# A local-attention layer pipelined over five engines: other token-block pairing, another PSUM bank and another engine for parts of the feed-forward norm, and a new order of work

## What is computed

```python
for i in range(6):
    x = attn_layer(shift_tokens(x), Wqkv[i], q_scale[i], k_scale[i], Wo[i]) + x
    x = ffn_layer(shift_tokens(x), ln_g[i], ln_b[i], W1[i], b1[i], W2[i], b2[i]) + x
# shift_tokens: the second half of the features comes from the token before
# attn_layer: q, k, v = x @ Wqkv; q and k to unit length per head, scaled, rotated;
#   each window of 32 attends to itself and the window before (masked softmax); @ Wo
# ffn_layer: xn = (x - mu) / sqrt(var + 1e-5) * g + b; a, gate = split(xn @ W1 + b1)
#   return a * gelu(gate) @ W2 + b2          (W1: 128 x 682, W2: 341 x 128)
```

## Time and profile before

| | |
|---|---|
| median of 3 runs | 4047.65 us (4046.55 to 4050.84) |
| the profiled execution | 4048.09 us, its span 4046.3 us |
| TensorE busy | 3729.9 us, 92% of the span |
| VectorE busy | 3487.8 us, 86% |
| ScalarE busy | 3422.3 us, 85% |
| GpSimd busy | 2387.8 us, 59% |
| mean granted TensorE clock | 0.982 of full |

### The profile page before, as it was taken

How to read it: one execution, slowest core, us unless ns; L and a number is a source line. 1 busy time by engine, 2 the same in 40 slices (tenths; PEclk the granted TensorE clock), 3 DMA queues, 4 the chain that set the end, 5 groups by cost and what they waited for, 6 DMA issues and landing times.

```text
span 4046.3 us, 125302 instructions
## 1 busy us (share of the span) xinstructions
PE 3729.9 (92%) x49248; PEld 2338.2 (58%) x49248; DVE 3487.8 (86%) x7192; ACT 3422.3 (85%) x9269; POOL 2387.8 (59%) x1420
## 2 busy tenths in 40 slices
PE   5999999967999999999999999999999999998987
PEld 2444444434666666666666666666666666666665
...
GB/s 50 8 9 9 9 9 36 1 0 50 80 76 77 90 85 81 75 80 86 87 82 74 80 77 95 85 77 77 76 98 80 79 76 75 98 82 79 76 82 56
DMA packets 158791, 263.19 MB, mean 65 GB/s; under 512 B 45696, under 2 KB 72064, under 8 KB 157952
## 3 DMA queue, kind: packets, MB, share of 16 engines
...
## 4 chain that ended last, share of the span: by engine, by line
PE 62%; DVE 18%; ACT 12%; issue 3%; POOL 2%; SPq 1%; DMA 1%; DVEq 0%; POOLq 0%; ACTq 0%
PE ps L655 17%; ACT arena L931 6%; PE ps L601 5%; PE ps L596 5%; PE ps L688 5%; PE ps L724 5%; PE ps L542 4%; PE ps L733 4%; PE ps L762 3%; PE ps L709 3%; PE ps L768 3%; DVE ssq L1164 3%; PE ps L537 3%; PE ps L775 3%; DVE arena L1147 2%
## 5 line engine op out<-in xcount | busy, mean ns | idle before, releaser
L655 PE MATMUL ps<-WB,arena 128*128 128x512 f32 x2304 | 1110.5, 605 | 132.5 <-DVE arena L1244 61.4
L931 ACT ACTIVATE arena<-arena,nmx 128x64 f32<-128x64 f32 x3072 | 1020.1, 337 | 4.4 <-DVE arena L1222 3.8
L475 POOL TENSOR_TENSOR arena<-arena 128x1024 f32<-128x1024 f32 x192 | 454.4, 2367 | 516.3 <-DVE arena L1147 516.0
L655 PEld LDWEIGHTS ps<-WB,arena 128*128 128x128 f32 x2304 | 399.9, 192 | 463.2 <-issue 438.8
L907 ACT ACTIVATE arena<-ps 128x1024 f32<-128x1024 f32 x384 | 393.5, 1025 | 314.1 <-PE ps L655 307.7
L491 POOL TENSOR_TENSOR arena<-arena,rinv 128x1024 f32<-128x1024 f32 x192 | 365.2, 1902 | 389.9 <-DVE rinv L1195 389.9
L931 ACT ACTIVATION_READ_ACCUMULATOR arena<-arena,nmx 128x1 f32 x3072 | 584.3, 190 | 0.0
L1141 DVE TENSOR_TENSOR arena<-ps,tables 128x1024 f32<-128x1024 f32 x384 | 464.7, 1210 | 87.4 <-ACT arena L907 87.4
L688 PEld LDWEIGHTS ps<-ident,arena 128*128 128x128 f32 x3072 | 355.6, 141 | 239.1 <-issue 173.6
L1147 DVE TENSOR_TENSOR arena<-ps,tables 128x512 f32<-128x512 f32 x768 | 489.9, 678 | 0.0
L480 POOL TENSOR_TENSOR arena<-arena 128x1024 f32<-128x1024 f32 x192 | 455.1, 2371 | 30.8 <-DVE arena L1147 30.8
...
## 6 DMA issues: line engine op xcount, KB each, us to landing
arena<-arena SPq DMA_DIRECT2D x768, 128.0 KB, 2.3
...
WB<-wb SPq DMA_DIRECT2D x24, 512.0 KB, 5.0
...
arena<-Y SPq DMA_DIRECT2D x96, 128.0 KB, 2.4
...
```

Of the source, the lines that this page charges most:

```text
L475: pool.tensor_tensor(tu[:, K], t1[:, K], t2[:, K], ALU.add).then_inc(addk_r, 1)
L655: i = pe.matmul(banks[:, c, :], xs_[t % RING], WB[:, w * INNER + c * COL:w * INNER + (c + 1) * COL], start=True, stop=True)
L931: i = act.activation(pe3[:, :, h, :], sc[:, 64 * h:64 * h + 64].rearrange("p (k q) -> p k q", k=2), ACT.Exp, bias=nmx[:, h:h + 1], accum_o ...
```

## The change

1. **Block pairing.** Side 0 serves blocks 0 and 2, side 1 blocks 1 and 3. Side 1 then needs the tile's values as they are, so `values` is one copy of 128 rows; side 0 needs them with the last 32 rows from the tile before, which two DMAs build. `outputs` writes in runs of 32 floats instead of 64.
2. **Bank.** The feed-forward's turn, back and down use bank 7 (attention's second output bank) between `outputs` of a tile and `attend` of the next. Gate and value products stay in banks 2 and 3. The waits move from `queries_of` to `attend`.
3. **Norm.** The unit step moves from VectorE to ScalarE, as scale and shift; VectorE adds one negation of the means, GpSimd one product.
4. **Order.** All five lists are reordered: attention's products come right behind the keys' of the next step, the value copy behind twelve of the sixteen exponents, the last four exponents between the second and the third gelu, the sine part of K before the cosine part. `add_k` and `add_q` are split over two steps. Weights of a new layer are issued behind `vshift` and `ff_in`. Feed-forward lags grow by one.

```diff
-        FF_BANK = 2, 3
+        FF_BANK, FO_BANK = (2, 3), 7
...
-                    q, o = slice(WIN * w, WIN * (w + 1)), (WIN * w + 64) % P
-                    here = slice((w % 2) * COL, (w % 2 + 1) * COL)
-                    sp.dma_start(PTw[q, w // 2, here], pt[q, COL:2 * COL]).then_inc(wide_in, 16)
+                    q, o = slice(WIN * w, WIN * (w + 1)), (WIN * w + 96) % P
+                    here = slice((w // 2) * COL, (w // 2 + 1) * COL)
+                    sp.dma_start(PTw[q, w % 2, here], pt[q, COL:2 * COL]).then_inc(wide_in, 16)
...
-                for dst, side, src, row, held in ((64, 0, (t - 1) % RING, 96, 1), (96, 0, r, 0, 0), (0, 1, r, 32, 0),
-                                                  (32, 1, r, 64, 1)):
-                    sp.dma_start(vv[r][dst:dst + WIN, side, :], vv[src][row:row + WIN, held, :])\
-                        .then_inc(vs_in, 16)
+                sp.dma_start(vv[r][0:96, 0, :], vv[r][0:96, 1, :]).then_inc(vs_in, 16)
+                sp.dma_start(vv[r][96:P, 0, :], vv[(t - 1) % RING][96:P, 1, :]).then_inc(vs_in, 16)
...
             def queries_of(t):
-                need(pe, rotq_r, t)
-                for q, lag, count, each in ((chunk(t - 2, 7), 7, fn_r, 1), (chunk(t - 2, 8), 8, xn_r, 1),
-                                            (chunk(t - 2, 9), 9, hf_r, MF), (chunk(t - 2, 10), 10, fin_r, 1)):
-                    if q is not None:
-                        pe.wait_ge(count, each * (q + 1))
+                need(pe, rotq_r, 2 * t)
+                q = chunk(t - 2, 10)
+                if q is not None:
+                    pe.wait_ge(hf_r, MF * (q + 1))
...
             def attend(t):
+                for q, count in ((chunk(t + 2, 8), fn_r), (chunk(t + 2, 9), xn_r), (chunk(t + 2, 11), fin_r)):
+                    if q is not None:
+                        pe.wait_ge(count, q + 1)
...
-            def values(t, side):
-                rows = slice(64 * side, 64 * side + 64)
-                i = act.activation(vv[t % RING][rows, side, :], kv_ps[rows].rearrange("p b c -> p (b c)"), ACT.Copy)
+            def values(t):
+                act.wait_ge(v_mm, t + 1)
+                need(act, vs_in, 32 * (t - 1))
+                act.activation(vv[t % RING][:, 1, :], kv_ps.rearrange("p b c -> p (b c)"), ACT.Copy).then_inc(v_r, 1)
+
+            def ff_unit(q):
+                act.wait_ge(frs_r, 2 * q + 2)
+                for j in range(PER):
+                    i = act.activation(fx[:, j * P:(j + 1) * P], ps[:, FO_BANK, j * P:(j + 1) * P], ACT.Identity,
+                                       bias=shift[:, j:j + 1], scale=rstd[:, 0, j:j + 1])
+                i.then_inc(fn_r, 1)
```

230 lines of the change are left out of this document (116 added, 114 removed).

## The result

The changed kernel takes **4025.7 us** (median of 6 runs, 4022.7 to 4035.6) against 4050.3 (6 runs, 4046.6 to 4051.4): a ratio of 0.9944, 95% interval 0.9932 to 0.9957. It is faster, by 24.6 us or 0.6%, small but clear of the scatter, where 88 us were forecast. The profiled execution has a span of 4021.9 us. Its page, first part: busy us, share of the span, instructions.

The account below looks back on a forecast made before the run. A ring of waits through ScalarE's value copy, not one full engine, was taken to bound the new order. From 4048.09 us: -98 for groups, +7.5 for layers, +3 for the end, about -88, so 3960; range 3928 to 4034.

Parts of the forecast that it names:

- the ring: Plain step: key products through attention, ScalarE's copies and exponents to the value copy, which releases the next key product: 13.64 us.
- (a): Rival, gate step between gelu 1 and 2: added table switches cost double, 63.5 per group, about 4062 us; chance 0.07.
- (e): Rival, value copy: one copy over 128 partitions costs like two, 2.03 us; group 64.3, about 4105 us; chance 0.02.
- (b): Rival, attention's products: the "issue" stall stays in full, hidden nowhere; group 62.3, about 4008 us; chance 0.14.
- (c): Rival, back step: VectorE closes its own ring, transpose waits for GpSimd's scaling; group 62.8, about 4033 us; chance 0.09.
- signs of being right: Key products in three of four steps idle 1 to 1.2 us for the value copy; group near 61.3; TensorE's work unchanged.
- signs of being wrong: Down-step query product released by VectorE's hidden product, transpose by GpSimd, attention's products by a DMA, or groups below 60.5.
- -2.04, times 48 is -98: Main term: each group of four tiles falls from 63.34 to 61.3 us, over 48 groups.
- Such an operation took 0.75 beside GpSimd: VectorE's added scaling of the mean, turn step: taken as 0.2, upper end 0.8, not charged because VectorE waits for exponents.
- I take 0.2: Per-group charge for the 1.18 us "issue" stall inside attention's products, bounds 0 and 1.2.
- +7.5: Five layer changes: key product waits for later-issued weights, 4.3 us lost per layer against 2.8 before, +1.5 each.
- bounds 0 and +6, taken as +3: End of the kernel: same chain with one stage moved, at most one group's gate and value products no longer beside attention.

Follow-up runs that it names:

- Experiments 13 and 14: Changed kernel with the scaling of the mean moved from VectorE to GpSimd: 4023.3 us; with the addition to the variance moved there too: 4016.6 us.
- Experiment 9: Changed kernel with the end reordered: gate and value products of the last chunk but one ahead of the last tile's attention: 4012.3 us.
- experiment 1: Changed kernel with a new layer's key and query weights issued right behind the widening DMAs again: 4011.1 us.

## Why the prediction was right in direction and wrong in size

**Right.** The single copy over 128 rows costs half, a table switch 1.28, TensorE's work is unchanged, and the value copy closes the ring in the new order. Turn, gate and down step came out at 13.78, 18.7 and 15.15 against 13.64, 18.50 and 15.25. Table switches (a) and the full-price copy (e) were rightly set low: the gelu starts 0.02 us behind the load, with no drain.

The 4025.7 us lie in the stated range, 3928 to 4034, because it was drawn to hold rivals (b) and (c), and mechanisms of both were at work; as a forecast of 3960 it missed by 66. Of the signs of being right, one failed: the value copy holds the key product in two steps of the group, by about 0.6 us, and not in three by 1 to 1.2. Of the signs of being wrong one came: a transpose released by GpSimd.

**The step that failed first: "-2.04, times 48 is -98".** Measured: -1.35 undisturbed and +0.28 of what lies beyond (13.5 over 47.75), -1.07 in all. The missing 0.97 are, up to rounding, 0.29 of the starting point, 0.38 of one small operation, 0.20 of other links by which the steps are longer than laid out (0.14 of it in the turn step), and 0.08 beyond the 0.2 that were taken for stalls. The last is small only because two things cancel: the groups between lose 0.54 more than before, the first and last ones 0.26 less, which the forecast didn't have.

- The group it started from, 63.34 us, is the typical one but not an undisturbed one: 63.05 is. The 0.29 between them is scattered stall or the like (the 35 groups between lose 0.32 each), and I counted it among what the new ring would save: 14 us. A laid-out ring knows no stalls, so it must be set against a group without any, and the stalls carried over as a term of their own.
- "Such an operation took 0.75 beside GpSimd; I ... charge neither, because in that step VectorE waits for the exponents anyway." The scaling of the mean took 1.22 us, and the cover was not there: the mask starts right behind the roots, at 16.6 from the step's key product, later than the 16.3 laid out. Late roots made GpSimd's scaling of the keys late, behind which stands that of the probabilities; it ends at 2080.37, the transpose starts 0.03 later, 6.8 into the back step and not 6.4, and the exponents follow at 8.1 and not 7.67. This is rival (c)'s link, a transpose waiting for GpSimd, at 0.31 us rather than the 1.5 of the earlier trace rows. Experiments 13 and 14 show it: take both small operations away, and the back step is 13.78. That is 0.38 per group, 18 us. The row that I used for the price, 754 ns, was itself such a wait: in the trace of before that operation starts at 2003.58 and ends at 2004.33, GpSimd's scaling of the keys at 2004.31. It was no price of an operation but what was left of another engine's. The two rows of before:

```profile
2003.58 0.75 DVE L1239 TENSOR_SCALAR ve<-mv 128x4 f32<-128x4 f32 x1
2002.41 1.90 POOL L491 TENSOR_TENSOR arena<-arena,rinv 128x1024 f32<-128x1024 f32 x1 [2.04 <-DVE rinv L1195]
```

**The issue stalls: "I take 0.2".** The term, 10 us, was too small. In the 35 groups between, 37.0 us or 1.06 a group lie beyond the undisturbed group, where 11.2 or 0.32 lay before, with as much stalling (23.6 against 24.4 us). The sum of the scattered part (+13.5) looks like the forecast's 10 only because the last 19 tiles gained 10 us, for a reason that no run looks into. The reason given for hiding, "it falls in the 1.15 us that TensorE now waits for the value copy", failed in its size: the copy is awaited for only 0.5 to 0.7 us, in two steps, and a stall is up to 2.5. The 1.15 was laid out for a plain step, and the group has none: the turn and the back step each have 0.6 us of the feed-forward's own turns in that place, as the layout itself says of the turn step. "There are now gaps in which the fetch can catch up" failed as well, since scores are still 256 instructions without one. Rival (b), stalls in full and hidden nowhere, 1.2 a group, had both the mechanism and about the size.

**Layers: +7.5, measured +12.0.** The mechanism was right: TensorE waits 3.7 to 4.1 us for weights, five times. Before, 3.6 us were lost at each and not the 2.8 taken, and after 6.0 and not 4.3, since some fetch stalls fall into these groups too. Issued early, the weights are there, and the tables on VectorE are next.

**End: "bounds 0 and +6, taken as +3", measured +13.3.** The step that failed was "the same chain with one stage moved". The stage moved behind the last tile's attention, which itself waits 3.8 us for its transfers; so the gate step stood between that attention and the last chunk's turn, with nothing beside it, and at half the granted clock at first (0.50 behind that wait). Experiment 9 returns 8.1. Of the other 5.2, by its trace against that of before, 4.0 lie between the last sum of squares and the last chunk's turn, and 0.9 between that turn and the turn back (5.58 us against 4.71), where the norm now runs through GpSimd and ScalarE. No experiment varied either.

**Two sums of the rivals.** In (a) 63.5 per group is 0.16 above 63.34, which is +8 and not +4. "14.65 in three steps", behind the 64 for two copies and the 64.3 of (e), is not laid out: 14.65 in the turn and the back step with 18.50 and 15.25 makes 63.1, and 64.3 is 61.3 with 1.0 added three times. With two copies the group took 64.99, since the gate and the down step grew too, by 0.5 and 1.03.

**What paid.** "The single value copy is what pays" holds only in the new order. In the old one it gives nothing, the norm on ScalarE 12.5 and both 20.6 us. In the new order neither can be missed: with two copies it is 121 us slower than before, with the norm on VectorE 23.

Left open: the last 5 us of the end, where the stalls were hidden before, why the last 19 tiles gained 10 us, and why experiment 1 lost a third less to scattered stalls than the changed kernel although both share the instruction count of TensorE; small shifts in time may decide whether a stall is covered, and that was not tried.
